# A new table of order for the attention block: statistics and normalisation a sample ahead, other evacuations, 50 of 64 mask tiles on GpSimd, one operand buffer per parity

## The reference

```
x = ln(src) * (1 + scale) + shift
q, k, v = (x @ W + b, split in 16 heads)
scores = q k^T / 4 + attention_bias        # 8 x 16 x 512 x 512, float32
probs  = softmax(where(src_mask, -inf, scores))
x = x + (concat(probs @ v) @ Wo + bo)      # the residual is the scaled, shifted x
h = ln(x) * g2 + beta2
x = x + gelu2(h @ W1 + b1) @ W2 + b2
```

## Time and profile before

| | us |
|---|---|
| median of 3 runs | 1039.73 |
| lowest, highest | 1037.82, 1042.37 |
| span of the profiled execution | 1036.6 |
| median minus span (what lies around it) | 3.1 |
| first transposition of sample 0 | 41.28 |
| first transposition of sample 1 | 125.05 |
| first transposition of sample 6 | 544.81 |
| first transposition of sample 7 | 629.11 |
| last transposition of attention | 709.50 |

### The profile page before, as it was taken

How to read it: one execution, slowest core, us unless ns; L and a number is a source line. 1 busy time by engine, 2 the same in 40 slices (tenths; PEclk the granted TensorE clock), 3 DMA queues, 4 the chain that set the end, 5 groups by cost and what they waited for, 6 DMA issues and landing times. The chain is left out here.

```text
span 1036.6 us, 20438 instructions
## 1 busy us (share of the span) xinstructions
PE 956.1 (92%) x5892; PEld 640.9 (62%) x5892; DVE 813.7 (78%) x2075; ACT 734.7 (71%) x1211; POOL 726.3 (70%) x596
## 2 busy tenths in 40 slices
PE   5879999999999999999999999898999999999963
PEld 4646556656655655755665665454777777777752
DVE  8887797878879879879787887874456877887697
ACT  3577887888798788788788878875446556655433
POOL 3487697788788878878778878777555567755631
PEclk9989999999999999999999999999999999999987
DMA  7978978997996997897799799752111111111001
GB/s 262 334 289 292 381 289 278 363 347 238 346 384 214 336 386 257 291 390 292 265 372 343 237 348 370 252 193 82 41 41 41 42 33 50 42 41 41 21 21 41
DMA packets 127535, 230.33 MB, mean 222 GB/s; under 512 B 5488, under 2 KB 53872, under 8 KB 123632
## 3 DMA queue, kind: packets, MB, share of 16 engines
q1 hardware_dynamic: 127472, 229.60, 62.0%
HBM read 187.63 MB, written 41.94 MB: 221 GB/s over the span
## 5 line engine op out<-in xcount | busy, mean ns | idle before, releaser
L937 ACT ACTIVATE prob<-prob,nmax 128x512 f32<-128x512 f32 x512 | 357.0, 729 | 59.6 <-DVE nmax L762 56.4
L762 DVE CUSTOM_DVE_ANT_0 prob<-s_bank,big 128x512 f32<-128x512 f32 x512 | 338.7, 684 | 69.7 <-POOL big L1101 40.3
L1101 POOL TENSOR_TENSOR big<-big,mterm_early 128x2048 f32<-128x2048 f32 (+2 forms) x88 | 305.3, 3484 | 71.5 <-DMA big<-in_fside_Bx16xSxS 62.3
L593 PEld LDWEIGHTS t_bank<-ident,prob 128*128 128x128 f32 x2048 | 238.1, 141 | 168.3 <-issue 51.5
L593 PE MATMUL t_bank<-ident,prob 128*128 128x128 f32 x2048 | 317.7, 278 | 15.9 <-ACT prob L937 6.7
L944 ACT COPY pt<-t_bank 128x512 f32<-128x512 f32 x312 | 181.1, 584 | 51.7 <-PE t_bank L593 50.6
L581 PE MATMUL s_bank<-stack_k,stack_q 128*128 128x512 bf16 x512 | 195.4, 382 | 1.3 <-DVE nmax L762 0.7
L771 DVE COPY pt<-t_bank 128x512 f32<-128x512 f32 x200 | 137.2, 686 | 34.9 <-PE t_bank L593 34.6
L2052 POOL TENSOR_TENSOR gl<-big,gh 128x512 fp32r<-128x512 f32 x64 | 84.6, 1329 | 69.8 <-DVE gh L1643 69.8
L607 PE MATMUL o_bank<-pt,val 128*32 128x512 f32 x1024 | 122.9, 598 | 1.2 <-ACT pt L944 0.7
L1905 ACT ACTIVATE big<-bank,late 128x512 f32<-128x512 f32 x62 | 42.7, 689 | 75.2 <-PE bank L1446 71.4
(11 more groups left out here) (257 smaller groups left out, 1610.0 us busy)
## 6 DMA issues: line engine op xcount, KB each, us to landing
big<-in_fside_Bx16xSxS SPq DMA_DIRECT2D x128, 1024.0 KB, 8.0
pieces_dram<-pieces SPq DMA_DIRECT2D x64, 384.0 KB, 7.3
stack_q<-pieces_dram SPq DMA_DIRECT2D x15, 1024.0 KB, 8.3
stack_k<-pieces_dram SPq DMA_DIRECT2D x15, 1024.0 KB, 10.0
pieces_dram<-pieces SPq DMA_DIRECT2D x32, 256.0 KB, 7.6
xin<-in_x SPq DMA_DIRECT2D x8, 512.0 KB, 8.7
x_dram<-x SPq DMA_DIRECT2D x8, 512.0 KB, 2.6
x1r<-x_dram SPq DMA_DIRECT2D x8, 512.0 KB, 4.3
```

The costliest lines, as they stand in the source:

```text
L593: last = pe.transpose(t_bank[n % 2][:, c * P:(c + 1) * P], prob[:, n % NT, c * P:(c + 1) * P], ident[:])
L762: dve.tensor_tensor_reduce(out=prob[:, n % NT, :], in0=s_bank[n % 3][:, :], in1=bias[:, h % NB, t, :], scale=-1.0, scalar=3e38, op0=ALU.ad ...
L937: act.activation(tile, tile, ACT.Exp, bias=nmax[:, n % NT:n % NT + 1], scale=-1.0).then_inc(exped.sem, 1)
L1101: pool.tensor_tensor(bias[:, h % NB, tiles], bias[:, h % NB, tiles], mterm[:, tiles], ALU.add).then_inc(masked.sem, 1)
```

## The change

The tables of order are new, and some work is made in another way:

```diff
-POOL_TILES = (0, 4, 2, 4, 3, 4, 4, 2, 4, 4, 0, 0, 2, 4, 2, 4)
+POOL_TILES = (0, 4, 2, 4, 4, 4, 4, 4, 3, 4, 1, 4, 4, 4, 1, 3)
-MASK_AT = (-6, 1, 3, 7, 10, 15, 19, 20, 25, 46, 48, 49, 54)
+MASK_AT = (-3, 2, 10, 18, 18, 18, 20, 20, 24, 25, 27, 27, 34, 38, 40)
-HEADS_OF_LOADS = dict(x1=3, first=2, expert=4, W1=6, mask=5, store_0=7, store_1=11)
-STACK_0_AT, STACK_1_AT = (9, 10), (0, 1)
-STATISTICS_AT, DEVIATION_AT, NORMALISE_AT = 11, 12, 14
-WEIGH_AFTER = 17
+HEADS_OF_LOADS = dict(x=3, x1=3, first=2, expert=4, W1=6, mask=5, store_0=8, store_1=13)
+STACK_0_AT, STACK_1_AT = (11, 12), (2, 4)
+STATISTICS_AT, AGGREGATE_AT, ROOT_AT, NORMALISE_AT = (23, 27, 34, 35), 36, 37, (51, 58, 62, 63)
+FIRST_STATISTICS_AT, FIRST_ROOT_AT, FIRST_NORMALISE_AT = 3, 5, (8, 9, 10, 11)
+WEIGH_AFTER, WEIGH_MORE = 17, 3
-VALUES_AT = (39, 41, 56)
-RESIDUAL_AT = 15
-EARLY_TERM_AT = QT * EARLY_HEADS
-LATE_TERM_AT = 12
-HIGH_STEP, LOW_STEP = 19, 20
+VALUES_AT = (58, 59, 62)
+TERM_AT = 53
+HIGH_STEP, LOW_STEP = 16, 20
-TAIL = [("O", 3, 6, 1), ("C", 0, 7, 1), ("C", 1, 9, 1), ("W", 0, 10, 1), ("W", 1, 12, 1)]
-AHEAD = [("XT", 0, 14, 0), ("XT", 1, 15, 0), ("Q", 0, 21, 0), ("K", 0, 23, 0), ("Q", 1, 28, 0), ("K", 1, 29, 0)]
-VALUES = [("V", 0, 31, 0), ("V", 1, 37, 0)]
-GROUPS = [("O", 0, 34, 0), ("O", 1, 42, 0), ("O", 2, 54, 0)]
+TAIL = [("O", 3, 6, 1), ("C", 0, 7, 1), ("C", 1, 8, 1), ("W", 0, 10, 1), ("W", 1, 13, 1)]
+AHEAD = [("XT", 0, 14, 0), ("XT", 1, 15, 0), ("Q", 0, 22, 0), ("K", 0, 25, 0), ("Q", 1, 28, 0), ("K", 1, 41, 0)]
+VALUES = [("V", 0, 45, 0), ("V", 1, 57, 0)]
+GROUPS = [("O", 0, 32, 0), ("O", 1, 44, 0), ("O", 2, 59, 0)]
-DVE_TAKES = (3, 7, 8, 12, 14, 17, 21, 22, 23, 25, 27, 30, 31, 34, 35, 36, 38, 40, 44, 46, 49, 51, 55, 57, 60)
+DVE_TAKES = (0, 2, 4, 7, 8, 9, 10, 13, 16, 21, 23, 25, 26, 28, 29, 30, 35, 36, 38, 40, 41, 43, 46, 48, 52, 54, 61)
...
+            def normalise_tile(b, t):
+                if t == 0:
+                    dve.wait_ge(root_done.sem, root_done.at(b, 1))
+                done = dve.tensor_scalar(xin[:, t], xin[:, t], mv[:, t, 0:1], rstd[:, t:t + 1], ALU.subtract, ALU.mult)
+                if t == QT - 1:
+                    done.then_inc(xhat_done.sem, 1)
...
+            def inverse_root(b):
+                pool.wait_ge(shifted.sem, shifted.at(b, 1))
+                apart(pool, k["apart"])
+                pool.tensor_tensor(rstd[:], std[:], minus_half[:], ALU.pow).then_inc(root_done.sem, 1)
...
+            def mask_term(b, t):
+                if t == 0:
+                    pool.wait_ge(mask_in.sem, mask_in.at(b, 16))
+                    if b > 0:
+                        pool.wait_ge(scored.sem, scored.at(b - 1, STEPS))
+                        pool.wait_ge(masked.sem, masked.at(b - 1, len(POOL_HEADS)))
+                apart(pool, k["apart"])
                 pool.tensor_scalar(
-                    mterm_late[:, t, :], mraw[:, t, :], MASKED, 0.0, ALU.mult, ALU.add
-                ).then_inc(late_term.sem, 1)
+                    mterms[(b + 1) % 2][:, t, :], mraw[:, t, :], MASKED, 0.0, ALU.mult, ALU.add
+                ).then_inc(term_done.sem, 1)
```

More of the change, by code:

```diff
@@ L268, in parts, with first_use @@
     return 2 if what in "QKVW" else 1
-def firsts(first, h, t):
-    return [t for n in range(QT * first, QT * h) if n % QT == t and t >= POOL_TILES[n // QT]]
+def first_use(h, t):
+    return all(t < tiles for tiles in POOL_TILES[:h])
 class SpareBanks:
@@ L495, in load_expert, with iteration @@
                              d["experts"][bass.ds(e, 1)].rearrange("e p l a -> (e p) (l a)")).then_inc(k["chosen"], 16)
-            def iteration(b, first=False, last=False):
-                if not last and not first:
-                    load_x(b)
+            def iteration(b, first=False, last=False, before_last=False):
                 for h in range(H):
@@ L518, in iteration @@
                         sp.dma_start(w1_raw, v["W1"]).then_inc(k["w1_in"], 16)
+                    if h == HEADS_OF_LOADS["x"] and not last and not before_last:
+                        load_x(b + 1)
                     if h == HEADS_OF_LOADS["mask"] and not last:
@@ L579, in scores @@
                 bank = s_bank[n % 3][:, :]
[L580 removed]
                 last = pe.matmul(bank, stack_q[:, h, t * P:(t + 1) * P], stack_k[:, h, :], start=True, stop=not by_pe)
                 if by_pe:
[L583 removed]
+                    last = pe.matmul(bank, ident_bf[:], mterms[b % 2][:, t, :], start=False, stop=True)
                 last.then_inc(scored.sem, 1)
@@ L689, in iteration @@
                     g, c = (n - WEIGH_AFTER) // 16, (n - WEIGH_AFTER) % 16
-                    if c in (0, 2) and (g >= 0 or not first):
-                        for part in (c, c + 1):
+                    if c in (0, WEIGH_MORE) and (g >= 0 or not first):
+                        for part in (0, 1) if c == 0 else (2, 3):
                             weigh(b if g >= 0 else b - 1, g % NG, part)
@@ L737, in _ @@
             iteration(0, first=True)
-            with pe.Fori(1, B - 1) as b:
+            for b in range(1, B - 1):
                 iteration(b)
@@ L819, in spare_use @@
                 elif what == "XT":
-                    if i == 0 and not first:
-                        dve.wait_ge(res_done.sem, res_done.at(b - 1, 1))
                     if banks.kind == "last":
@@ L855, in iteration @@
                         take_turned(b, n - 1)
-                    if not last and n == STATISTICS_AT:
-                        statistics(b)
-                    if not last and n == NORMALISE_AT:
-                        normalise(b)
+                    if first and n == FIRST_STATISTICS_AT:
+                        for t in range(QT):
+                            statistics_of(b, t)
+                        aggregate(b)
+                    if first and n in FIRST_NORMALISE_AT:
+                        normalise_tile(b, FIRST_NORMALISE_AT.index(n))
+                    if ahead and n in STATISTICS_AT:
+                        statistics_of(b + 1, STATISTICS_AT.index(n))
+                    if ahead and n == AGGREGATE_AT:
+                        aggregate(b + 1)
+                    if ahead and n in NORMALISE_AT:
+                        normalise_tile(b + 1, NORMALISE_AT.index(n))
                     if last and n == NORMALISE_LAST:
@@ L993, in iteration @@
                         take_turned(b, n - 1)
-                    if n == (DEVIATION_LAST if last else DEVIATION_AT):
+                    if last and n == DEVIATION_LAST:
                         deviation(b)
@@ L1026, in _ @@
             iteration(0, first=True)
-            with act.Fori(1, B - 1) as b:
+            for b in range(1, B - 1):
                 iteration(b)
@@ L1177, in iteration @@
                         copy_values(b - 1, NG - 1)
-                    if n == RESIDUAL_AT and not first:
-                        keep_residual(b - 1)
+                    if n == FIRST_ROOT_AT and first:
+                        inverse_root(b)
+                    if n == ROOT_AT and not last and not before_last:
+                        inverse_root(b + 1)
                     if not last and n in CUT_STEPS:
@@ L1207, in _ @@
             iteration(0, first=True)
-            before = links[0]
-            with pool.Fori(1, B - 1) as b:
+            for b in range(1, B - 2):
                 iteration(b)
-            assert links[0] - before == per_link
+            iteration(B - 2, before_last=True)
             iteration(B - 1, last=True)
```

176 lines of the change are left out of this document (74 added, 102 removed).

## The result

| | before | after |
|---|---|---|
| median, runs on the same chip (6 each), us | 1040.38 | 1049.01 |
| lowest to highest | 1036.67 to 1042.37 | 1047.97 to 1051.74 |
| span of the profiled execution | 1036.6 | 1047.8 |

The ratio of after to before is 1.0079, with a 95% interval from 1.0045 to 1.0112: slower by 0.8%. The forecast was 1015.5.

A forecast was written before the change was run, and what follows sets the result against it. TensorE was taken as the bound, its own work 92% of a middle sample's 83.95 us. Savings of 16.5 (samples 1 to 6), 5.8 (sample 0) and 2.0 (sample 7) gave span 1012.3, plus 3.1: 1015.5, range 999 to 1036.

The forecast's parts named there:

- XT's wait for the normalisation: Largest TensorE stall of a middle sample before, 1.7 us for the step; forecast to go with the norm made ahead.
- the forecast of 81.2 for a middle sample: Sum 75.8 + 1.2 + 2.2 + 2.0 us, 2.75 less than the 83.95 measured before.
- Norm a sample ahead: Term for the earlier norm: XT's wait of 1.7 us goes, ScalarE falls to 65.9, VectorE rises to about 71.
- absorbed by this room: The statistics' instructions (0.41 us) and epsilon's addition cost nothing, covered by room on ScalarE and VectorE.
- half of the norm's part: In sample 0, this half of the earlier norm's gain is lost to masks, leaving it 5.8 us shorter, at 78.0.
- Normalisation in four places: Four separate tiles on VectorE each may wait for GpSimd's masks: about 7 us a sample, 2.0 reaching TensorE.
- The sign that it gave for being wrong: TensorE's steps after 51 or at 0 to 2 over 2 us longer, or VectorE's mask waits over 8 a sample.
- ledger: TensorE's own work added up from step-to-step distances: 77.3 us a middle sample before, 75.8 forecast after.
- 1.2 + 2.2: Middle sample: 1.2 us fixed unevenness of plain steps plus 2.2 of stalls left in plain runs (between 1 and 4).
- the third, slower: Rival: normalising tiles hold VectorE uncovered; over 6 us a sample reaching TensorE turns the sign, 8 gives 1052; chance 0.12.
- GpSimd paces: Rival: loads land late, GpSimd's masks hold each other back, a middle sample stays about 83.3 us, total 1031; chance 0.20.
- The first rival: VectorE's lead hides all the tiles' waits: a middle sample takes 79.2 us, total 1001; chance 0.18.

The follow-up runs named there:

- e1: The changed kernel with the addition of epsilon moved from VectorE to GpSimd: 1042.51 us, ratio to before 1.0023.
- e5: The changed kernel with epsilon on GpSimd and the normalising tiles of samples ahead on ScalarE: 1013.84 us, ratio to before 0.9752.
- e2: The changed kernel with the normalising tiles of samples ahead on ScalarE, and two small instructions more on GpSimd: 1031.36 us, ratio to before 0.9903.
- e10: The changed kernel with only the low half's subtraction moved from VectorE to GpSimd: 1036.52 us, ratio to before 0.9941.
- e3: The changed kernel with the four normalising tiles together again on VectorE, at step 59 (step 8 in sample 0): 1041.06 us, ratio to before 1.0012.
- e6: The changed kernel with epsilon and the low half on GpSimd and the normalising tiles of samples ahead on ScalarE: 1011.35 us, ratio to before 0.9722.
- e11: The changed kernel with epsilon and low half on GpSimd, tiles on ScalarE, and head 13 masked by GpSimd in two tiles, not four: 998.76 us, ratio 0.9581.
- e8: The kernel before with one dead epsilon addition on VectorE at step 46 of samples 0 to 6, beside a mask: 1055.45 us, ratio 1.0126.
- e9: The kernel before with one dead reciprocal on VectorE at step 46 of samples 0 to 6, beside a mask: 1040.95 us, ratio 0.9996.
- e7: The changed kernel with epsilon and low half on GpSimd, the four tiles together on VectorE at step 59 (8 in sample 0): 1019.41 us, ratio 0.9816.
- e4: The changed kernel with the old distribution of masks, 43 mask tiles on GpSimd instead of 50: 1041.90 us, ratio to before 1.0004.

## Why the prediction was wrong

**Right.** TensorE's own work in a sample fell to 75.8: steps with and without a mask matmul still lie 0.215 apart. XT's wait for the normalisation, W's wait behind C's evacuation and the table loads in samples 0 to 6 are gone. Sample 7 came out at 77.6 (78.4 forecast), and sample 6, without the norm ahead, at 80.6: the forecast of 81.2 for a middle sample describes a kernel in which the norm costs nothing beyond 2.0. The inverse root on GpSimd took 1.02.

**The step that failed** is that of three VectorE instructions that wait for GpSimd only the normalising tiles were priced, and in sample 0 even these by a guess. In the prediction's terms: in "*Norm a sample ahead*", "the addition of epsilon" was "absorbed by this room"; the low half has no term at all; and in the sum, sample 0 has "half of the norm's part again lost to masks".

"*Normalisation in four places*" itself held in mechanism, and was sized too high: 7.0 of waiting a sample (3.0, 0.3, 4), measured 4.1; 2.0 reaching TensorE, measured 1.29 (step 1, behind the tile of step 62). The sign that it gave for being wrong, steps longer by over 2 after 51 or at 0 to 2, didn't come: step 1 grew by 1.2 and step 61 by 0.6. By the same step distances, two other steps are over their ledger: 23 by 1.66 (the low half) and 38 by 2.55 (epsilon), medians of samples 1 to 6. On average over these samples, of which the last has no epsilon, the three are 1.3, 1.6 and 2.0, 4.9 together: 2.9 more a sample than the 2.0 forecast. The other terms nearly close: of the mean of samples 1 to 6, 84.66, the ledger's 75.8 and the 4.9 leave 4.0, of which 0.97 is step 61 (the next sample's first scores) and 0.7 are steps at half clock behind the stalls. The forecast had 1.2 + 2.2 = 3.4 for all of that.

- *Epsilon* was named beside the statistics' 0.41 and given no price. It is a tensor_scalar from SBUF to SBUF like the tiles, and the rule that I applied to the tiles asks for the form, not for the size. It took 3.06 on average, and was worth 6.5 us of the kernel's time with the tiles in place (e1) and 17.5 without them (e5 against e2).
- *The low half* (`LOW_STEP`) was not costed. It stands in the diff only as a step that did not change, 20. But the masks moved beside it: its two instructions took 2.0 together before and 3.5 to 4.8 after, in samples 1 to 6. e10 gives 12.5 back, with a shorter epsilon in it.
- *Sample 0* was forecast 5.8 shorter and came out 9.7 longer, 15.5 of the total miss of 35.5. I took "half of the norm's part" as lost to masks, from no row. Laying GpSimd's queue beside steps 8 to 11 as I did for the middle gives three masks in a row and a tile in each: three waits of the tiles instead of the one of the earlier trace rows. e2 and e3 give 11 to 12 us of it back.
- *The clock* was no term of the sum. In samples 3 and 5 the stall of 2.4 at step 38 was followed by some 3 us at half clock. The mean granted clock is 0.98 in samples 1, 3 and 5 and 1.00 in 2 and 4, and those three took 85.9 on average against 84.8. In sample 0 it was over 11.5 us in one piece; by an estimate from the mean clocks (0.89 of 93.49, 0.96 of 83.77) some 21 us were at half clock, against 7 before.

Against the rivals: the third, slower, has the direction and the cause, a lock on VectorE, but 1049 is near its price of 1052 by luck. Its condition, over 6 of the tiles' waiting reaching TensorE in each sample, didn't come: they give 1.3, and epsilon, the low half and sample 0, which it doesn't name, give the rest. "GpSimd paces" is refuted for the changed kernel by the waits (1.7 for masks in the middle) and in part true for e6. The first rival's price of 1001 for hidden waits is near what e11 reaches (998.8) when they are taken away, which suggests that the rest of the change is worth about its forecast gain; but e11 also has two masks fewer on GpSimd and the tiles on ScalarE, and e6, with the change's own masks, took 1011.4.

The Trainium skill, "SBUF — State Buffer", section "Who interferes with whom", sets out which VectorE instructions can share an interface with GpSimd: tensor_scalar in a two-port mode, for the whole instruction, and any instruction with two SBUF inputs while GpSimd reads. By that rule epsilon and both L816 instructions were to be suspected beforehand, and the trace agrees with all three and with e8. The page lists neither the reciprocal nor the statistics among the forms that can wait; e9 and the statistics' 0.42 (at most 0.43 in 32) agree.

**Open.** The larger part of e5's 11 beyond e1 and e2 is the tiles' longer waits in e1, as said there; how much of the rest is less time at half clock wasn't isolated. The stall of 0.97 at step 61, which the versions of e5, e6 and e11 have as well, was not tried, but the trace shows what it waits for:
```profile
387.60 0.38 PE L574 MATMUL s_bank<-stack_k,stack_q 128*128 128x512 bf16 x1 [0.81 <-DVE nmax L755]
```
These are the next sample's first scores. The scores rotate through three banks and a sample has 64 steps, so `scores` lets them wait for the bias addition of the step just before, 63, where the others wait for one three or four steps back. The change puts VectorE's work for V (57) and O (59) ahead of that addition; before, with other steps for both, the stall was 0.36. That these cause the growth is argued, not shown.

## What to carry to other kernels

Before a small instruction is moved or split, ask of its form whether it can wait for GpSimd, and lay GpSimd's timeline beside its new place: its price is what is left of the GpSimd instruction that it meets, whatever its own size. Instructions of such a form belong on ScalarE, on GpSimd itself, or where GpSimd idles; a group on VectorE meets one long instruction once, but waits for short ones each time, and holds back all that stands behind it (e3, e7). What is taken off one such place can lengthen the wait at the next (e1), so a single removal tells less than a pair. Work moved to GpSimd can give VectorE more to wait for (e4). Then count each stall of TensorE with the half clock that may follow it.

## What the runs showed of the hardware

- A tensor_scalar of 128 x 4 numbers took 0.17 alone, and 2.0 to 3.4 beside a GpSimd tensor_tensor of 4.1 (e8 and the changed kernel, 13 cases); it ended 0.02 to 0.03 us behind it each time. A reciprocal of the same size and place took 0.17.
- Four tensor_scalars of 128 x 256 in a row took 0.40 each alone, and up to 0.84 each beside GpSimd instructions of 0.62 (e3, e7).
- GpSimd's own instruction, once begun, isn't visibly lengthened: the mask beside the 3.24 took 8.12 for two, against 4.10 for one elsewhere, and all 50 of this size in samples 1 to 5 took 4.08 to 4.14. No run isolates what GpSimd does when VectorE has begun first.
- The same 2.40 idle of TensorE at step 38 was followed by a granted clock of 0.50 in sample 3 (1.2 GHz) and of 1.00 (2.4 GHz) in samples 2 and 4.
